# One activation of 2000 columns in place of two of 1000: the exponential of two neighbouring chunks

## The reference

```python
scores = jnp.einsum('hbnd,hbdm->hbnm', f_self, f_other)
masked = a_h * scores
masked = jnp.where(masked >= 0, masked, 0.2 * masked)
masked = masked / jnp.sqrt(jnp.float32(ATT))            # ATT = 16
masked = masked + jnp.where(a_h == 0, jnp.float32(-1000000000.0), jnp.float32(0.0))
attn = jax.nn.softmax(masked, axis=-1)
...
node_features = jnp.einsum('bhnm,bhmo->bhno', attn, feats)
```

## Time and profile before

| | |
|---|---|
| median of 3 runs | 1613.17 us (1610.61 to 1616.14) |
| the profiled execution, its time | 1614.31 us |
| its span, from the first to the last instruction | 1612.5 us |
| mean granted TensorE clock | 0.950 of full speed |
| busy: PE / DVE / ACT / POOL | 84% / 80% / 77% / 66% of the span |
| exponentials (L731) | 576, 595.4 us together |
| slopes (L723) | 576, 574.2 us together |

### The profile page before, as it was taken

How to read it: one execution, slowest core, us unless ns; L and a number is a source line. 1 busy time by engine, 2 the same in 40 slices (tenths; PEclk the granted TensorE clock), 3 DMA queues, 4 the chain that set the end, 5 groups by cost and what they waited for, 6 DMA issues and landing times.

```text
span 1612.5 us, 21612 instructions
## 1 busy us (share of the span) xinstructions
PE 1357.4 (84%) x7440; PEld 666.8 (41%) x7440; DVE 1291.0 (80%) x1561; ACT 1238.0 (77%) x1475; POOL 1068.3 (66%) x571
## 2 busy tenths in 40 slices
PE   3377889898999988988989989899889888899766
PEld 2143434444444443444444444344444444344323
DVE  1367878888888888988888888888888888988865
ACT  1268889888798778878887878888888887878731
POOL 2036776777676876778667876768767786867422
PEclk9989999999999999999999999999999999999867
DMA  9535351434334244334425344334424253300000
GB/s 85 84 56 85 36 93 43 70 55 51 73 65 71 32 63 83 53 57 54 76 47 88 38 56 87 45 66 50 76 53 69 51 51 67 56 13 16 25 10 10
DMA packets 144979, 91.14 MB, mean 57 GB/s; under 512 B 102420, under 2 KB 132570, under 8 KB 144858
## 3 DMA queue, kind: packets, MB, share of 16 engines
q1 hardware_dynamic: 129766, 71.01, 21.6%
q0 software_dynamic: 13904, 18.12, 14.6%
q10 hardware_dynamic: 1200, 0.63, 0.2%
HBM read 103.33 MB, written 21.38 MB: 77 GB/s over the span
## 4 chain that ended last, share of the span: by engine, by line
PE 38%; DVE 20%; ACT 14%; issue 14%; POOL 8%; SPq 3%; DMA 2%; ACTq 0%; POOLq 0%; DVEq 0%
DVE RUN L874 9%; PE M L640 8%; PE M L597 7%; ACT LS L723 7%; PE Z L558 6%; PE Z L560 6%; POOL LS L469 5%; ACT LS L731 5%; PE Z L571 4%; DVE LS L888 3%; PE Z L650 2%; SPq L345 2%; PE Z L703 2%; POOL RSTD L474 1%; SPq L324 1%
## 5 line engine op out<-in xcount | busy, mean ns | idle before, releaser
L469 POOL TENSOR_TENSOR LS<-LS,MB 125x1000 f32<-125x1000 f32 x372 | 862.4, 2334 | 446.8 <-DVE LS L888 285.3
L874 DVE TENSOR_TENSOR RUN<-Z,RUN 125x1000 f32<-125x1000 f32 x528 | 631.7, 1196 | 173.7 <-ACT LS L723 159.5
L723 ACT ACTIVATE LS<-Z 125x1000 f32<-125x1000 f32 x576 | 574.2, 997 | 152.5 <-PE Z L560 151.5
L731 ACT ACTIVATE LS<-LS 125x1000 f32<-125x1000 f32 x576 | 595.4, 1035 | 63.2 <-POOL LS L469 39.2
L558 PE MATMUL Z<-AT,BI 126*125 126x500 fp8e4 x1152 | 365.4, 400 | 113.5 <-DVE RUN L874 64.9
L597 PE MATMUL M<-LS,V 125*18 125x500 f32 x2304 | 314.2, 619 | 70.8 <-ACT LS L731 68.7
L560 PE MATMUL Z<-FS,FO 96*125 96x500 bf16 x1152 | 352.5, 388 | 0.0
L888 DVE TENSOR_TENSOR LS<-LS,MB 125x1000 f32<-125x1000 f32 x204 | 282.7, 1390 | 7.5 <-DMA MB<-row_maxima 1.3
L558 PEld LDWEIGHTS Z<-AT,BI 126*125 126x125 bf16 x1152 | 136.7, 141 | 273.0 <-DVE RUN L874 137.7
L560 PEld LDWEIGHTS Z<-FS,FO 96*125 96x125 bf16 x1152 | 163.1, 142 | 94.4 <-issue 12.5
L640 PE MATMUL M<-AT,XP 125*128 125x500 fp8e4 x756 | 194.3, 380 | 0.0
(11 more groups left out here) (115 smaller groups left out, 862.8 us busy)
## 6 DMA issues: line engine op xcount, KB each, us to landing
MB<-row_maxima SPq DMA_DIRECT2D x48, 500.0 KB, 4.0
adj_cast<-in_adj_dram POOLq DMA_DIRECT2D x96, 183.1 KB, 4.4
FO<-PARTS SPq DMA_DIRECT2D x192, 46.9 KB, 2.1
FS<-PARTS SPq DMA_DIRECT2D x180, 46.9 KB, 2.1
XP<-in_x_dram SPq DMA_DIRECT2D x8, 336.0 KB
XA<-in_x_dram SPq DMA_DIRECT2D x8, 336.0 KB
out_dram<-X SPq DMA_DIRECT2D x7, 375.0 KB
AT<-adj_cast SPq DMA_TRANSPOSE x144, 3.1
```

The lines of the kernel that those rows point to most:

```text
L469: nc.gpsimd.tensor_tensor(rows, rows, MB[:P, u % 2, :, :], ALU.subtract).then_inc(sub_pool, 1)
L723: nc.scalar.activation(LS[:P, q % RL, :, :], banks("Z", q)[:P], ACT.Prelu, alpha=0.2).then_inc(bent, 1)
L731: nc.scalar.activation(rows, rows, ACT.Exp, scale=0.25).then_inc(exps, 1)
L874: nc.vector.tensor_tensor(run, z, run, ALU.max).then_inc(maxed, 1)
```

## The change

`expo` is called once for each pair of chunks, at the odd step, and works on two neighbouring slots of `LS` with one activation of 2000 columns. It waits for the subtractions of both chunks, on both engines' semaphores. `weigh(w)` waits for w + 1 exponentials in place of 2w + 2. Nothing else is touched: the same values are computed, and `bend`, `maximum`, `subtract` and `weigh` stay at their steps.

```diff
--- before.py
+++ after.py
@@ -590,7 +590,7 @@
                     pe.wait_ge(o4_ready, u + 1)
                     if i == 0:
                         pe.wait_ge(v_ready, NS * (b + 1))
-                pe.wait_ge(exps, 2 * w + 2)
+                pe.wait_ge(exps, w + 1)
                 for n in range(4):
                     par, hh = divmod(n, 2)
                     e = 2 * w + par
@@ -722,12 +722,11 @@
                     act.wait_ge(weighed, (q - RL) // 2 + 1)
                 nc.scalar.activation(LS[:P, q % RL, :, :], banks("Z", q)[:P], ACT.Prelu, alpha=0.2).then_inc(bent, 1)
 
-            def expo(e):
-                if by_vector(e):
-                    act.wait_ge(sub_dve, by_dve(e) + 1)
-                else:
-                    act.wait_ge(sub_pool, by_pool(e) + 1)
-                rows = LS[:P, e % RL, :, :]
+            def expo(w):
+
+                act.wait_ge(sub_dve, by_dve(2 * w + 2))
+                act.wait_ge(sub_pool, by_pool(2 * w + 2))
+                rows = LS[:P, 2 * w % RL:2 * w % RL + 2, :, :]
                 nc.scalar.activation(rows, rows, ACT.Exp, scale=0.25).then_inc(exps, 1)
 
             def bend_maxima(u):
@@ -831,8 +830,8 @@
                 at = layer_at(q, HIGH)
                 if at and at[1] < 3:
                     high(*at)
-                if 0 <= q - EXP_AT < QN:
-                    expo(q - EXP_AT)
+                if 0 <= q - EXP_AT < QN and (q - EXP_AT) % 2:
+                    expo((q - EXP_AT) // 2)
                 if turned_at(q - 1) is not None:
                     bend_maxima(turned_at(q - 1))
```

## The result

The changed kernel takes 1643.26 us (median of 4 runs, 1637.29 to 1645.86) against 1614.66 us of the kernel before (4 runs): a ratio of 1.0157 with a 95% interval of 1.0133 to 1.018. It is slower by 28.6 us in the medians, where 15 us faster was forecast.

What follows compares the result with a forecast made beforehand. No single bound: a ring of engines waiting for one another, TensorE holding 38% of the chain. Terms of -37, -4 and +26 gave -15 us against 1614.3: 1599 us, its own range 1580 to 1608, 8 in 10 from 1572 to 1632.

Steps and rivals of the forecast that it cites:

- term 1: ScalarE's odd slope starts 0.90 us sooner once the even exponential leaves its place ahead of it: -37 us.
- term 3: On ScalarE a held pair's exponentials end up to 0.81 us later, delaying the next even slope and the weighing: +26 us.
- term 2: Fewer activation starts on ScalarE, one exponential of 1.85 us for each pair: -4 us.
- 41 of the 80 places: Pairs on the old chain whose next link is VectorE's maximum (29) or copy `O` (12), each credited 0.90 us.
- the wait of the degrees for `O`: TensorE's degrees wait 23.4 us for ScalarE's copy of finished sums; shorter waits were to show the odd slope's gain.
- The bound on the other side: The next even slope, which is not moved, sets the pace anyway, so the odd slope's gain is 0.
- The sign named for it: ScalarE's busy time was to fall by about 63 us, with idle time in its place.
- The rival that came true: The double exponential holds ScalarE for 1.85 us against ready even slopes and weighings: 1639 us, chance 0.23.
- The point from which it was to decide: The blocking rival decides once fewer than 24 of 41 places keep their 0.90 us.
- What costs nothing: At the main loop's end the last double exponential ends 0.81 us later, covered by VectorE's norm; otherwise 0.8 us.
- The signs: Profile changes named beforehand; weighing waits over 40 us longer, or VectorE's waits for slopes not falling, would refute the forecast.

Runs made afterwards that it cites:

- term 1 alone: Kernel before, all exponentials single, the even one moved from ahead of the odd slope to directly behind it, ahead of the short work: 1603.18 us, ratio 0.9925.
- two singles: Kernel before, with a pair's two exponentials of 1000 columns back to back behind the odd step's short work: 1639.78 us, ratio 1.015.

## Why the prediction was wrong

Two steps failed. By the runs, and as far as terms add, 25 of the some 44 us between forecast and result lie in term 1 and some 11 in term 3; the rest is term 2's 4 us and what the terms do not add up to. Either one put right alone would not have given the result: with term 1 at -12 the sum is +10 us, with term 3 at +37 it is -4.

**Term 1, the odd slope sooner, was mis-sized**: 37 us forecast, 12 us measured by itself. I counted 41 of the 80 places of the old chain in full. The run of term 1 alone shows why that was too much. By the same count over its timeline, VectorE's waits ahead of odd chunks fell from 67.2 to 15.3 us, but those ahead of even chunks rose from 92.4 to 128.6 us, and the odd slopes now wait 49.9 us for their scores (11.2 before). The even slope is not sooner, and most of what the odd one gains is waited off there, or was never there for want of scores. Nor did the wait of the degrees for `O`, for which 12 of the 41 places were counted, get shorter (25.4 us, 23.4 before). The bound on the other side, that the even slope sets the pace, was the nearer.

**Term 2 was right in its durations**: 1.868 us for 1.85. What it is worth in time could not be told from nothing (4 us forecast). The sign named for it was wrong: ScalarE's busy time fell by 19 us, not 63. Time in which two neighbours overlap counts once in the busy time, so the overlap of the earlier trace rows should have come off there as well. From the even slope at 711.70 to the next at 715.23 a pair without waits takes 3.53 us, where it took 3.62; 288 times that difference is 26 us, much nearer.

**Term 3, the pair that ends later, is the second step that failed.** It was rightly seen as a mechanism, at the right place, and priced too low: +26 us. The runs show some 37 us, twice: as the cost of the place behind the short work, and as that of merging the 151 pairs with it. The fault was to count only those late weighings and slopes that lay on the old chain (37 places). Going through the pairs one by one, each from its own old start, had found 64 late weighings worth 38 us, and I let the chain throw out 57 of them as covered. The chain is that of the kernel before. Once the weighing is late TensorE's queue stops there, the matmuls behind it are late, ScalarE's copies that wait for them are late, and the next pair stands behind the copies. The weighing's wait rose by 74 us, in 115 waits where there were 70. That lateness goes round in this way is shown for the feature steps by the chain, and there half of it at each turn; for the other short work it is argued from the place at 709.17. Over all 151 pairs 37 us are 0.25 us a pair, under a third of the 0.83 us by which the exponential is longer: the lateness is paid in part, but at many more places than the old chain ran through.

**The rival that came true** is the first, the double exponential that blocks, with 1639 us against 1643.26 measured, and its terms (a quarter of term 1, the late weighings in full: 9 and 38 us) are near the 12 and 37 us that the runs give. But its name was wrong: it is the place behind the odd step's short work, not the length of the instruction, since two singles at that place lose the same and the doubles without short work lose nothing. The point from which it was to decide, fewer than 24 of 41 places kept, was passed: 12 us are 13 places.

**What costs nothing** was not tested by a run of its own, and the profile speaks against it in part: the last slope starts 24.9 us later (1532.3 against 1507.4 us), the last exponential ends 29.1 us later (1574.96 against 1545.85 us), and the span is 27.2 us longer. Some 4 us were lost behind the last slope, where 0.8 us at most was foreseen, and some 2 us of them came back. **The signs** did their part: the weighing's wait grown by over 40 us was named as what would prove the forecast wrong, with VectorE's waits not falling as the second, and both came. VectorE's waits are also fewer and left mostly ahead of even chunks, as was said. But the wait of the degrees for `O`, which did get shorter (3.3 us, 23.4 before), was no sign of term 1: with term 1 alone it stays at 25.4 us, while with the two singles, where the weighing is late, it is 3.2 us: a TensorE that is late itself comes to it later.

One place looks like a part of the loss. In the second graph the changed kernel loses about 5 us at one step, where GpSimd waits for the spread maxima (timeline of the changed kernel):

```profile
229.04 0.21 ACT L737 ACTIVATE LMAX<-RMAX 125x8 f32<-125x8 f32 x1
...
229.52 4.53 SPq L324 DMA_DIRECT2D FS<-PARTS  x6
...
234.15 1.01 SPq L360 DMA_DIRECT2D row_maxima<-LMAX  x2
...
240.47 10.05 POOL L469 TENSOR_TENSOR LS<-LS,MB 125x1000 f32<-125x1000 f32 x4 [4.38 <-DMA MB<-row_maxima]
```

The maxima were ready at 229.25, and SP's queue was still issuing loads of `FS` until 234.05. In the kernel before those loads were over when the maxima came, and GpSimd waited 1.19 us. But the kernel with term 1 alone, faster than the kernel before, waits as long at the same step, and that of the two singles, which loses as much as the change, waits 1.19 us; the two in order:

```profile
234.36 7.78 POOL L469 TENSOR_TENSOR LS<-LS,MB 125x1000 f32<-125x1000 f32 x3 [4.74 <-DMA MB<-row_maxima]
```

```profile
237.74 4.59 POOL L469 TENSOR_TENSOR LS<-LS,MB 125x1000 f32<-125x1000 f32 x2 [1.19 <-issue]
```

So this wait does not part the kernels that lose from those that gain, and is not what makes the change slower.

One thing goes along with the loss and was not separated from it. TensorE's mean granted clock is 0.944 in the profile of the change and 0.950 in that of the kernel before, and the same 7440 matmuls are busy for 1367.8 us in place of 1357.4. In the run of the two singles it is 0.939 and 1374.9 us, in that of term 1 alone 0.955 and 1352.1 us. Longer matmuls can thus be up to 10 of the change's 27 us; whether the lower clock only follows from TensorE's longer waits, no run here tells.

## What to carry to other kernels

An instruction that fills a wait on its engine and is needed late looks like pure cost on the chain, but where it is moved to decides: ask what stands ahead of it there, and what that waits for. When a consumer is made late, follow its engine's queue on until you are back at the instruction you moved; if you get there, a lateness can come round again, in part at least (half of it at each turn here), whether or not the chain of the kernel before ran through it. And split a change by the places it touches: merged only where the step held no other work, this loss of 1.6% became a gain of 0.5%, and the part of the change that gained, the order, gave 0.75% without any merging.

## What was not expected of the hardware

Nothing in how the chip ran single instructions. The activation of 2000 columns took what one of 1000 took plus (1868 - 1035) / 1000 = 0.833 ns a column, and the control runs were unexpected only in the kernel's stagger: one step more for the weighing cost 4.9%, and copies that come one exponential (1.035 us) later cost 3.7%.
